# Expert blocks of a mixture-of-experts stage: gathered token rows in six buffers in place of three

## The chip, the cores and the metric

The kernel runs on one core of a Trainium2 chip. The metric is the device time of one execution in microseconds (us); below, KB means 1024 bytes and MB a million, as the profile counts them.

## The reference

The reference is a chain of eight layers on N = 3125 nodes of D = 256 features, all in float32: four graph layers over 50000 edges, and four mixture-of-experts layers. Three of the experts' layers matter here. Cut down, the first of them is:

```python
# layer L0_ffn: 16 experts, 2 chosen, width 512 (F)
topk_vals, topk_idx = jax.lax.top_k(x @ gate_w + gate_b, 2)
topk_w = jax.nn.softmax(topk_vals, axis=-1)
h = relu(einsum('bsh,ehf->bsef', x, w1) + b1)
expert_out = einsum('bsef,efh->bseh', h, w2) + b2
moe = sum(topk_w[..., None] * take(expert_out, topk_idx))
```

L2_ffn has 8 experts of width 1024, of which each token takes one, up to a capacity of 489 tokens an expert. L3_ffn has 6 experts, two chosen, with three matrices each (256 to 256 to 256 to 256).

## The kernel before

The kernel does not compute every expert for every token. `route` sorts the (token, expert) pairs by expert into blocks of BR = 250 rows, each block of one expert, and writes two lists: `token_i`, which token's row each slot of a block takes, and `to_i`, where its answer goes. `block_experts` (line 1442) then works through the blocks. It is called three times, and the text calls its stages by letters:

- **stage A**, L0_ffn: 40 blocks, weights of 1026 KB a block, stage start near 1584 us of the span;
- **stage B**, L2_ffn: 16 blocks, weights of 2052 KB a block, near 5272 us;
- **stage C**, L3_ffn: 30 blocks, weights of 770 KB a block, near 6390 us.

In each stage a block of 250 rows is two half-blocks of 125 (TB = 2), and each engine runs its own program, held together by semaphores:

- **SyncE** (line 1494) loads for block n the weights `w` and the second bias `b2` (125 KB, broadcast over the partitions) into one of three buffers. From block 3 on it first waits until block n-3 has its answers (`o_done`).
- **GpSimd** (line 1627) gathers and scatters. `gather(n)` (line 1637) issues two indirect DMAs, 125 rows of 1 KB each, from `tokens` in DRAM to `rows`. The buffer is chosen by n modulo R = 3, and from block 3 on the gather first waits until block n-3 has been transposed (`t_mm`). The scatter of block n (line 1655; line 1660 in stage B, a plain DMA) writes the two halves of `y` to `answered`, after `o_done` of block n. The loop over n (line 1649) is: gather block n + R, wait for `o_done` of block n, scatter block n. In stage A the last nine turns of the loop each also issue up to three small indirect DMAs `order_d`, 25 in all (line 1665); they belong to a sort for a later layer.
- **TensorE** (line 1504) transposes a block's rows (`turn`, line 1511, waits for `rows_in`), multiplies with the first matrix (`up`, line 1525, waits for `w_in`), in stage C with the middle one (`middle`, line 1534), and with the last (`down`, line 1544). It runs ahead: the order is

```python
for n in range(blocks):
    if FM: middle(n)
    if n + 1 < blocks: up(n + 1)
    if n + 2 < blocks: turn(n + 2)
    down(n)
```

- **ScalarE** evicts `hid` and `mid` (lines 1566, 1577); **VectorE** copies the transposed rows out of PSUM to `xT` (line 1587) and adds `b2` to the product to make `y` (line 1595). `y` has two buffers: VectorE waits until the scatter of block n-2 has landed (`stored`).

So the gather of block n+4 stands on GpSimd directly behind the scatter of block n, which waits for `down(n)`; and `down(n+2)` stands on TensorE behind `turn(n+4)`, which waits for that gather.

Of the kernel before, what the change touches and what calls it, by code (L numbers as in the profile page):

```python
# [17 lines left out]
N, D, E = 3125, 256, 50000  # L18
P = 125
# [18 lines left out]
def stage(k):  # L38

    return Stage(k)  # L40
# [336 lines left out]
def make_records(k, fld, slot_i, attr_t, m_w1, m_b1, m_w2, m_b2, noise):  # L377

    nc = k.nc
    K1, GE = 50, G * 128  # L380
    R = 3
    with stage(k) as s:
        attr = s.sb("attr", [K1, R, GE])
        pos, hid = s.sb("pos", [128, 2, 2, GE]), s.sb("hid", [128, 2, 2, GE])
        hs = s.sb("hs", [128, 2, 2, GE])
        rec = s.sb("rec", [128, R, G, RW])
        w1, b1 = s.sb("w1", [K1, D]), s.sb("b1", [128, 2])
# [3 lines left out]
            s.sem(n) for n in ("w_in", "hid_mm", "hid_act", "hid_exp", "hid_ln", "hs_done", "fil_mm", "rec_done"))  # L391
        attr_in, sent = ([s.sem(f"{n}{j}") for j in range(R)] for n in ("attr_in", "sent"))
        noise_in = s.sem("noise_in")
        with s.block() as block:
            @block.sync
            def _(sp):
# [7 lines left out]
                for g in range(NGR):  # L404
                    if g >= R:
                        sp.wait_ge(hid_mm, 2 * (g - R) + 2)
                    sp.dma_start(attr[:, g % R, :], attr_t[:, g * GE:(g + 1) * GE]).then_inc(attr_in[g % R], 16)
# [672 lines left out]
BR = 250  # L1080
# [361 lines left out]
def block_experts(k, table, token_i, result, block_i, x, blocks, sort=False, shift=None, to_i=None):  # L1442
# [5 lines left out]
    nc = k.nc  # L1448
    FC = x.f // 128
    FM = 2 if x.wm is not None else 0  # L1450
    TB = BR // P
    R = 3
    SEMS = 2
    EACH = 3
    FROM = blocks - NT // EACH - 1
# [9 lines left out]
    cleared = 0 if to_i is not None else 1  # L1465
    last_fill = lambda n: fill["mid", n, FM - 1] if FM else fill["up", n, FC - 1]
    with stage(k) as s:
        rows = s.sb("rows", [P, R, TB, D])
        xT = s.sb("xT", [128, 2, 2, BR])
        w, b2 = s.sb("w", [128, R, x.width]), s.sb("b2", [P, R, D])  # L1470
        part = lambda n, at, to: w[:, n % R, at:to]
# [8 lines left out]
        if FM:  # L1480
            mid = s.sb("mid", [128, 2, FM, BR])
        ps_t, ps_h, ps_o = s.ps("ps_t", [128, 2, 512]), s.ps("ps_h", [128, 4, 512]), s.ps("ps_o", [P, 2, 512])
        w_in, rows_in = ([s.sem(f"{n}{j}") for j in range(R)] for n in ("w_in", "rows_in"))
        stored = [s.sem(f"stored{b}") for b in range(2)]
        t_mm, t_ev, h_mm, h_sb, o_mm, o_done, made = (s.sem(n) for n in ("t_mm", "t_ev", "h_mm", "h_sb", "o_mm", "o_done", "made"))
        if sort:
# [5 lines left out]
        with s.block() as block:  # L1492
# [10 lines left out]
            @block.tensor  # L1503
            def _(pe):
                def turn(n):
                    pe.wait_ge(rows_in[n % R], 16 * TB * (n // R + 1))
                    if n >= 2:
                        pe.wait_ge(t_ev, n - 1)
                    for t in range(TB):
                        for half in range(2):  # L1510
                            ins = nc.tensor.transpose(ps_t[:, n % 2, half * BR + t * P:half * BR + (t + 1) * P], rows[:, n % R, t, half * 128:(half + 1) * 128], k.ident[0:P, 0:P])
                    ins.then_inc(t_mm, 1)

                def free(at):
                    if at >= 4:
                        pe.wait_ge(h_sb, at - 3)

                def up(n):
                    pe.wait_ge(w_in[n % R], 16 * SEMS * (n // R + 1))
                    pe.wait_ge(t_ev, n + 1)  # L1520
                    for f in range(FC):
                        at = fill["up", n, f]
                        free(at)
                        for c in range(2):
                            ins = nc.tensor.matmul(ps_h[:, at % 4, 0:BR], w1(n, c, f), xT[:, n % 2, c, :], start=c == 0, stop=c == 1)  # L1525
                        ins.then_inc(h_mm, 1)

                def middle(n):
                    pe.wait_ge(h_sb, fill["up", n, FC - 1] + 1)
                    for f in range(FM):  # L1530
                        at = fill["mid", n, f]
                        free(at)
                        for c in range(FC):
                            ins = nc.tensor.matmul(ps_h[:, at % 4, 0:BR], wm(n, c, f), hid[:, n % 2, c, :], start=c == 0, stop=c == FC - 1)
                        ins.then_inc(h_mm, 1)

                def down(n):
                    pe.wait_ge(h_sb, last_fill(n) + 1)
                    last, count = (mid, FM) if FM else (hid, FC)
                    for t in range(TB):  # L1540
                        if n:
                            pe.wait_ge(o_done, 2 * (n - 1) + t + 1)
                        for c in range(count):
                            ins = nc.tensor.matmul(ps_o[:, t, 0:D], last[:, n % 2, c, t * P:(t + 1) * P], w2(n, c), start=c == 0, stop=c == count - 1)
                        ins.then_inc(o_mm, 1)

                turn(0)
                turn(1)
                up(0)
                for n in range(blocks):  # L1550
                    if FM:
                        middle(n)
                    if n + 1 < blocks:
                        up(n + 1)
                    if n + 2 < blocks:
                        turn(n + 2)
                    down(n)

            @block.scalar
            def _(act):  # L1560
                def up(n):
                    act.wait_ge(w_in[n % R], 16 * SEMS * (n // R + 1))
                    for f in range(FC):
                        at = fill["up", n, f]
                        act.wait_ge(h_mm, at + 1)
                        nc.scalar.activation(hid[:, n % 2, f, :], ps_h[:, at % 4, 0:BR], x.func, bias=b1(n, f)).then_inc(h_sb, 1)  # L1566
# [15 lines left out]
            def _(dve):  # L1582
# [6 lines left out]
                def answers(n):  # L1589
                    dve.wait_ge(w_in[n % R], 16 * SEMS * (n // R + 1))  # L1590
                    if n // 2 + cleared:
# [36 lines left out]
            @block.gpsimd  # L1628
            def _(pool):
                if sort:  # L1630
                    nc.gpsimd.iota(ids[:], [[P, NT]], base=0, channel_multiplier=1).then_inc(ready, 1)
                    nc.gpsimd.memset(before[:], 1.0).then_inc(ready, 1)
                    pool.wait_ge(ready, 2)
                    nc.gpsimd.affine_select(out=before[:], in_=before[:], compare_op=ALU.is_gt, fill=0.0, base=0,
                                            pattern=[[-1, P]], channel_multiplier=1).then_inc(ready, 1)

                def gather(n):
                    if n >= R:
                        pool.wait_ge(t_mm, n - R + 1)
                    for t in range(TB):  # L1640
                        nc.gpsimd.indirect_dma_start(rows[:, n % R, t, :], None, table, bass.IndirectOffsetOnAxis(token_i[:, TB * n + t:TB * n + t + 1], 0)).then_inc(rows_in[n % R], 16)

                for n in range(R):
                    gather(n)
                pool.wait_ge(made, 1)
                for lo, hi in SPLIT[0:2 * cleared]:
                    for b in range(2):
                        pool.dma_start(result[blocks * BR + b * P + lo:blocks * BR + b * P + hi, :], zero[lo:hi, :]).then_inc(stored[b], 16)
                for n in range(blocks):
                    if n + R < blocks:  # L1650
                        gather(n + R)
                    pool.wait_ge(o_done, 2 * n + 2)
                    if to_i is not None:
                        for t in range(TB):
                            nc.gpsimd.indirect_dma_start(result, bass.IndirectOffsetOnAxis(to_i[:, TB * n + t:TB * n + t + 1], 0), y[:, n % 2, t, :], None,
                                                         bounds_check=2 * N - 1, oob_is_err=False).then_inc(stored[n % 2], 16)
                    else:
                        to = result[n * BR:(n + 1) * BR, :].rearrange("(t p) f -> p t f", p=P)
                        for lo, hi in SPLIT:
                            pool.dma_start(to[lo:hi], y[lo:hi, n % 2, :, :]).then_inc(stored[n % 2], 16)  # L1660
                    if sort and n >= FROM:
                        if n == FROM:
                            pool.wait_ge(ranked, 1)
                        for t in range(EACH * (n - FROM), min(EACH * (n - FROM + 1), NT)):
                            nc.gpsimd.indirect_dma_start(k.order_d, bass.IndirectOffsetOnAxis(k.rank_i[:, t:t + 1], 0), ids[:, t:t + 1], None).then_inc(ordered, 16)
                if sort:
                    pool.wait_ge(ordered, 16 * NT)
                for b in range(2):
                    pool.wait_ge(stored[b], 32 * (blocks // 2 + cleared))
# [1629 lines left out]
```

## Time and profile before

| | |
|---|---|
| median of 3 runs | 6747.97 us (6741.45 to 6748.28) |
| the profiled execution's own time | 6698.96 us |
| its span, first to last instruction | 6697.1 us |
| mean granted TensorE clock | 0.785 of full |
| busy: TensorE matmuls, VectorE, ScalarE, GpSimd | 67%, 50%, 38%, 46% of the span |
| mean DMA rate over the span | 109 GB/s |
| stages A, B, C, first gather to last scatter | about 385, 255 and 265 us |

Shares of the span are means over some thirty stages with different limits, so they say little on one stage. The rows further down are of the three stages alone. In a timeline a row gives the start, the length, the engine and line, and in brackets how long the engine had been idle before, and what ended that. A DMA instruction on GpSimd is the writing of its descriptors; the transfer goes on after it. "PEclk" is the clock granted to TensorE as a share of full speed.

### The profile page before, as it was taken

The numbers are of one execution on the slowest core, as the hardware profiler recorded it, in microseconds if no ns is written. First come the engines' busy times: TensorE is split into PE (matmuls) and PEld (weight loads), VectorE is DVE, ScalarE is ACT, GpSimd is POOL, SyncE is SP. The second block draws the span as 40 slices with busy tenths as digits, with TensorE's granted clock in tenths as the row PEclk, the third lists the DMA queues.
The fourth block names the chain that finished last, engine by engine and source line by source line (L and its number), as shares of the span: only waits on it lengthen the run. The fifth ranks groups of instructions, "written<-read, shape, count | busy, mean of one in ns | idle before, by whom it ended". The sixth has DMA issues, their size and how long they took to land. (4 is left out here: it accounts for less than half of the span.)

```text
span 6697.1 us, 62301 instructions
## 1 busy us (share of the span) xinstructions
PE 4506.5 (67%) x16614; PEld 3138.6 (47%) x16614; DVE 3363.6 (50%) x7195; ACT 2539.8 (38%) x5493; POOL 3081.5 (46%) x2991
## 2 busy tenths in 40 slices
PE   4799945556954777545556676996777592555665
PEld 2466634345743555212245343774555581333454
DVE  2344435554625666679744565225666315454522
ACT  2577723331212233355432443223333122666511
POOL 3276766652653666235500652004665124666244
PEclk7899966766986666679977788997777696677878
DMA  4433343334644555224330221004555353666245
GB/s 115 128 105 103 107 89 92 91 81 116 201 136 114 140 139 138 58 82 132 107 79 9 51 47 29 14 3 124 140 143 126 115 168 102 183 188 182 66 140 168
DMA packets 464743, 727.93 MB, mean 109 GB/s; under 512 B 173990, under 2 KB 334801, under 8 KB 453972
## 3 DMA queue, kind: packets, MB, share of 16 engines
q1 hardware_dynamic: 299372, 388.69, 20.0%
q0 software_dynamic: 161520, 330.66, 18.8%
q10 hardware_dynamic: 3530, 4.89, 0.2%
q8 instruction: 129, 2.11, 0.1%
q14 instruction: 192, 1.57, 0.1%
HBM read 592.07 MB, written 139.85 MB: 109 GB/s over the span
## 5 line engine op out<-in xcount | busy, mean ns | idle before, releaser
L593 PE MATMUL ps<-msg,same 128*125 128x256 f32 (+2 forms) x3328 | 1343.0, 548 | 883.9 <-issue 397.7
L593 PEld LDWEIGHTS ps<-msg,same 128*125 128x125 f32 x3328 | 773.1, 260 | 1297.8 <-issue 787.2
L569 POOL DMA_INDIRECT msg<-d_gat,src_i x832 | 794.1, 954 | 430.9 <-issue 197.0
L482 POOL DMA_INDIRECT rec<-rec,slot_i x391 | 415.8, 1063 | 299.5 <-PE ps_f L424 121.2
L569 POOL DMA_INDIRECT msg<-d_lin,src_i x416 | 394.2, 948 | 267.8 <-issue 101.9
L569 POOL DMA_INDIRECT msg<-rel_rows,src_rel x416 | 399.4, 960 | 213.5 <-issue 98.3
L645 ACT ACTIVATE same<-off 128x500 f32<-128x500 f32 x208 | 128.9, 620 | 865.8 <-PE ps L593 455.2
L424 PE MATMUL ps_f<-w,hs 128*128 128x256 f32 x1568 | 391.0, 406 | 27.1 <-DVE hs L462 26.3
L639 ACT ACTIVATE off<-ramp_r,minus_lo 128x125 f32<-128x125 f32 x1248 | 390.6, 384 | 10.9 <-PEq L58 10.9
L424 PEld LDWEIGHTS ps_f<-w,hs 128*128 128x128 f32 x1568 | 308.7, 202 | 145.8 <-DVE hs L462 74.9
L1566 ACT ACTIVATE hid<-ps_h,w 128x250 f32<-128x250 f32 x348 | 163.5, 470 | 531.8 <-PE ps_h L1525 508.6
L2642 PE MATMUL ps_y<-pr,ident 128*128 128x447 f32 (+1 forms) x448 | 212.6, 600 | 208.9 <-DVE pr L2693 208.9
L1525 PE MATMUL ps_h<-xT,w 128*128 128x250 f32 x1392 | 323.3, 387 | 28.0 <-DMA b<-in_L_ffn_b 27.8
L580 PEld LDWEIGHTS ps_v<-vt,pick 125*128 125x128 f32 x1664 | 290.0, 251 | 105.9 <-issue 86.5
L2632 POOL TENSOR_TENSOR dB<-rows,u 128x894 f32<-128x894 f32 (+1 forms) x112 | 215.3, 1924 | 230.0 <-DVE hh L2684 162.2
L2811 POOL DMA_INDIRECT msg<-d_small,idx x256 | 242.3, 946 | 161.0 <-DVE weighed L2914 84.9
L580 PE MATMUL ps_v<-vt,pick 125*128 x1664 | 271.2, 295 | 49.7 <-DVE pick L688 37.8
L1525 PEld LDWEIGHTS ps_h<-xT,w 128*128 128x128 f32 x1392 | 271.1, 196 | 70.5 <-DMA b<-in_L_ffn_b 37.1
L462 DVE SCALAR_TENSOR_TENSOR hs<-hid,pos 128x1024 f32<-128x1024 f32 x98 | 120.1, 1225 | 355.6 <-ACT hid L452 258.6
L2828 PE MATMUL ps<-spread,oh_lo 128*125 128x500 f32 x512 | 253.6, 654 | 66.6 <-DVE spread L2920 66.6
L717 DVE TENSOR_TENSOR agg_m<-agg_m,ps 125x256 f32 x416 | 174.7, 420 | 204.8 <-DMA got<-answered,slot_i 90.4
L717 DVE TENSOR_TENSOR x<-x,ps 125x256 f32 x416 | 174.6, 420 | 203.8 <-DMA rec<-blank,pad_i 75.1
(594 smaller groups left out, 9209.3 us busy)
## 6 DMA issues: line engine op xcount, KB each, us to landing
lo_rows<-lo_r SPq DMA_DIRECT2D x208, 256.0 KB
fil<-rec SPq DMA_DIRECT2D x104, 512.0 KB
rows<-bc_d SPq DMA_DIRECT2D x96, 447.0 KB
w<-in_L_ffn_packed SPq DMA_DIRECT2D x40, 1026.0 KB
w<-in_L_ffn_packed SPq DMA_DIRECT2D x16, 2052.0 KB
w<-in_L_ffn_packed SPq DMA_DIRECT2D x30, 770.0 KB
rel_rows<-row SPq DMA_DIRECT2D x25, 896.0 KB
lo_rows<-ffn_lo_r SPq DMA_DIRECT2D x32, 500.0 KB
```

What stands on the lines that cost most here:

```text
L424: ins = nc.tensor.matmul(ps_f[:, g % 2, j, :], hs[:, g % 2, c, j * 128:(j + 1) * 128], w2[:, c, :], start=c == 0, stop=c == 1)
L482: nc.gpsimd.indirect_dma_start(k.rec, bass.IndirectOffsetOnAxis(slot_i[0:rows, c:c + 1], 0), rec[0:rows, g % R, j, :], None).then_inc(sent ...
L569: nc.gpsimd.indirect_dma_start(msg[:, g % R, j, :], None, table, bass.IndirectOffsetOnAxis(idx[:, n:n + 1], 0)).then_inc(msg_in[g % R], 16)
L580: ins = nc.tensor.matmul(ps_v[:, g % 2, j * H2:(j + 1) * H2], pick[0:P, g % 2, j * 128:(j + 1) * 128], vt[:, ds(t, 1), :].rearrange("p t h ...
L593: nc.tensor.matmul(ps[:, j, 0:width], same[:, g % 2, j, :], msg[:, g % R, j, 0:width], start=True, stop=True).then_inc(mm, 1)
L639: ins = nc.scalar.activation(off[:, b, j, :], k.ramp_r1[:], ACT.Abs, bias=k.minus_lo1[:, n:n + 1])
L717: nc.vector.tensor_tensor(into, into, ps[:, j, 0:width], ALU.add).then_inc(added, 1)
L1525: ins = nc.tensor.matmul(ps_h[:, at % 4, 0:BR], w1(n, c, f), xT[:, n % 2, c, :], start=c == 0, stop=c == 1)
L2632: nc.gpsimd.tensor_tensor(dB[:, n % 3, :, 0:hi - lo], both(rows[:, n % R, 0, 0:hi - lo], hi - lo), u[:, :, lo:hi], ALU.mult).then_inc(ins_ ...
L2642: ins = nc.tensor.matmul(ps_y[:, h, 0:size(n)], k.ident[:], pr[:, n % 2, h, 0:size(n)], start=st == 0, stop=st == SN - 1)
L2811: nc.gpsimd.indirect_dma_start(msg[:, g % R, j, :], None, table, bass.IndirectOffsetOnAxis(idx[:, n:n + 1], 0)).then_inc(msg_in[g % R], 16)
L2828: nc.tensor.matmul(ps[:, 0:NT * W], oh_lo[:, g % 2, j, :], spread[:, g % 2, j, :], start=False, stop=False).then_inc(mm, 1)
```

## The change

`rows` gets a buffer count of its own, RR = 6, with a semaphore for each buffer, and everything that indexed `rows` or `rows_in` by R uses RR. The weights keep R = 3. On GpSimd six blocks are gathered ahead of the loop, and turn n of the loop gathers block n + 6, in place of n + 3, ahead of the scatter of block n. The buffer's wait becomes that for the transposition of block n - 6 of the gather's block. `rows` takes 12 KB of each partition in place of 6.

```diff
     R = 3
+    RR = 6
...
-        rows = s.sb("rows", [P, R, TB, D])
+        rows = s.sb("rows", [P, RR, TB, D])
...
-        w_in, rows_in = ([s.sem(f"{n}{j}") for j in range(R)] for n in ("w_in", "rows_in"))
+        w_in, rows_in = [s.sem(f"w_in{j}") for j in range(R)], [s.sem(f"rows_in{j}") for j in range(RR)]
...
-                    pe.wait_ge(rows_in[n % R], 16 * TB * (n // R + 1))
+                    pe.wait_ge(rows_in[n % RR], 16 * TB * (n // RR + 1))
...
                 def gather(n):
-                    if n >= R:
-                        pool.wait_ge(t_mm, n - R + 1)
+                    if n >= RR:
+                        pool.wait_ge(t_mm, n - RR + 1)
...
-                for n in range(R):
+                for n in range(RR):
                     gather(n)
...
                 for n in range(blocks):
-                    if n + R < blocks:
-                        gather(n + R)
+                    if n + RR < blocks:
+                        gather(n + RR)
                     pool.wait_ge(o_done, 2 * n + 2)
```

The order changes on GpSimd alone. At the start of stage A its program before is this (`rows<-tokens` is a gather of half a block, `answered<-y` a scatter of half a block):

```order
L1641 DMA rows<-tokens,token_i_16 125x256 x8
L1655 DMA answered<-y,to_i_16 6250x256 x2
L1641 DMA rows<-tokens,token_i_16 125x256 x2
L1655 DMA answered<-y,to_i_16 6250x256 x2
L1641 DMA rows<-tokens,token_i_16 125x256 x2
```

and with the change (its lines are one further down):

```order
L1642 DMA rows<-tokens,token_i_16 125x256 x14
L1656 DMA answered<-y,to_i_16 6250x256 x2
L1642 DMA rows<-tokens,token_i_16 125x256 x2
L1656 DMA answered<-y,to_i_16 6250x256 x2
L1642 DMA rows<-tokens,token_i_16 125x256 x2
```

Seven blocks are gathered ahead of the first scatter where four were; after that, scatters and gathers alternate as before. The end of stage C on GpSimd before:

```order
L1655 DMA answered<-y,to_i_6 6250x256 x2
L1641 DMA rows<-tokens,token_i_6 125x256 x2
L1655 DMA answered<-y,to_i_6 6250x256 x2
L1641 DMA rows<-tokens,token_i_6 125x256 x2
L1655 DMA answered<-y,to_i_6 6250x256 x8
```

and with the change:

```order
L1656 DMA answered<-y,to_i_6 6250x256 x2
L1642 DMA rows<-tokens,token_i_6 125x256 x2
L1656 DMA answered<-y,to_i_6 6250x256 x2
L1642 DMA rows<-tokens,token_i_6 125x256 x2
L1656 DMA answered<-y,to_i_6 6250x256 x14
```

The last gather stands ahead of the last seven blocks' scatters, where it stood ahead of the last four.

## Rows read from the trace of the kernel before

**Rows 1.** Waits of stage A, 1584 to 1968: us in total, times, longest.
```profile
PE ps_t L1511 <- DMA rows<-tokens,token_i: 35.8, 9, 15.2
PE ps_h L1525 <- DMA b<-in_L_ffn_b: 27.8, 16, 9.4
```
**Rows 2.** Waits of stage B, 5272 to 5530.
```profile
PE ps_t L1511 <- DMA rows<-tokens,token_i: 26.5, 2, 21.7
```
**Rows 3.** Waits of stage C, 6389 to 6662.
```profile
POOL answered L1655 <- DVE y L1595: 83.0, 17, 12.0
PE ps_t L1511 <- DMA rows<-tokens,token_i: 69.2, 15, 15.3
```
**Rows 4.** Windows: PE, PEld, DVE, ACT, POOL busy (count), PEclk, DMA share, GB/s.
```profile
1643.00:1880.00 237.00, 218.27 (x1030) 184.73 (x1028) 140.92 (x238) 53.15 (x114) 140.51 (x115) 0.98 0.66 199
1880.00:1970.00 90.00, 61.14 (x264) 50.96 (x264) 17.89 (x28) 13.16 (x28) 67.17 (x53) 0.88 0.38 101
6418.00:6655.00 237.00, 179.89 (x793) 152.88 (x791) 42.91 (x85) 53.57 (x114) 136.53 (x112) 0.91 0.53 161
...
5282.00:5292.00 10.00, 0.99 (x4) 0.71 (x4) 0.00 (x0) 0.00 (x0) 1.23 (x3) 0.50 1.02 325
```
**Rows 5.** Timeline of stage C, TensorE: turn, middle and up.
```profile
6444.52 1.10 PE L1511 MATMUL ps_t<-ident,rows 125*128 125x125 f32 x4 [4.03 <-DMA rows<-tokens,token_i]
...
6461.40 1.08 PE L1511 MATMUL ps_t<-ident,rows 125*128 125x125 f32 x4 [4.00 <-DMA rows<-tokens,token_i]
...
6465.29 1.85 PE L1534 MATMUL ps_h<-hid,w 128*128 128x250 f32 x8
...
6470.83 1.85 PE L1534 MATMUL ps_h<-hid,w 128*128 128x250 f32 x8
6472.52 1.85 PE L1525 MATMUL ps_h<-xT,w 128*128 128x250 f32 x8
```
**Rows 6.** Timeline of stage C, GpSimd: first scatter, one round, last scatter.
```profile
6418.55 1.24 POOL L1655 DMA_INDIRECT answered<-y,to_i  x1 [12.04 <-DVE y L1595]
...
6449.86 1.23 POOL L1655 DMA_INDIRECT answered<-y,to_i  x1 [4.99 <-DVE y L1595]
...
6452.91 1.23 POOL L1641 DMA_INDIRECT rows<-tokens,token_i  x1 [0.30 <-issue]
6454.44 1.22 POOL L1641 DMA_INDIRECT rows<-tokens,token_i  x1 [0.30 <-issue]
6455.97 1.23 POOL L1655 DMA_INDIRECT answered<-y,to_i  x1 [0.30 <-issue]
...
6652.51 1.19 POOL L1655 DMA_INDIRECT answered<-y,to_i  x1 [1.56 <-DVE y L1595]
```
**Rows 7.** Timeline of stage C, SyncE's queue: a load of weights.
```profile
6466.10 0.35 SPq L1500 DMA_DIRECT2D w<-in_L_ffn_packed  x1
```
**Rows 8.** Timeline of stage A, TensorE: turns of blocks 4, 5, 33 and 35.
```profile
1635.95 0.59 PE L1511 MATMUL ps_t<-ident,rows 125*128 125x125 f32 x4
...
1643.22 0.59 PE L1511 MATMUL ps_t<-ident,rows 125*128 125x125 f32 x4
...
1875.53 0.59 PE L1511 MATMUL ps_t<-ident,rows 125*128 125x125 f32 x4
...
1898.29 1.09 PE L1511 MATMUL ps_t<-ident,rows 125*128 125x125 f32 x4 [4.60 <-DMA rows<-tokens,token_i]
```
**Rows 9.** Timeline of stage A, GpSimd: scatter of block 31, its gather, the end.
```profile
1880.96 1.22 POOL L1655 DMA_INDIRECT answered<-y,to_i  x1 [1.46 <-DVE y L1595]
...
1884.01 1.19 POOL L1665 DMA_INDIRECT order_d<-ids,rank_i  x1 [0.30 <-issue]
...
1968.99 1.19 POOL L1665 DMA_INDIRECT order_d<-ids,rank_i  x1 [0.30 <-issue]
```
**Rows 10.** Timeline of a graph layer behind stage A, GpSimd: gathers in a row.
```profile
2088.33 1.19 POOL L569 DMA_INDIRECT msg<-d_gat,src_i  x1 [13.05 <-POOLq L58]
...
2122.44 0.95 POOL L569 DMA_INDIRECT msg<-d_gat,src_i  x1 [0.30 <-issue]
```

More of the change, by code:

```diff
@@ L1510, in turn @@
                         for half in range(2):
-                            ins = nc.tensor.transpose(ps_t[:, n % 2, half * BR + t * P:half * BR + (t + 1) * P], rows[:, n % R, t, half * 128:(half + 1) * 128], k.ident[0:P, 0:P])
+                            ins = nc.tensor.transpose(ps_t[:, n % 2, half * BR + t * P:half * BR + (t + 1) * P], rows[:, n % RR, t, half * 128:(half + 1) * 128], k.ident[0:P, 0:P])
                     ins.then_inc(t_mm, 1)
@@ L1637, in gather @@
                 def gather(n):
-                    if n >= R:
-                        pool.wait_ge(t_mm, n - R + 1)
+                    if n >= RR:
+                        pool.wait_ge(t_mm, n - RR + 1)
                     for t in range(TB):
-                        nc.gpsimd.indirect_dma_start(rows[:, n % R, t, :], None, table, bass.IndirectOffsetOnAxis(token_i[:, TB * n + t:TB * n + t + 1], 0)).then_inc(rows_in[n % R], 16)
-                for n in range(R):
+                        nc.gpsimd.indirect_dma_start(rows[:, n % RR, t, :], None, table, bass.IndirectOffsetOnAxis(token_i[:, TB * n + t:TB * n + t + 1], 0)).then_inc(rows_in[n % RR], 16)
+                for n in range(RR):
                     gather(n)
```

## The prediction

> **What bounds the kernel now.** The three stages are read in three views. First the waits of each stage, for what TensorE waits. In stage C it waited 69.2 us in 15 places for gathered rows [rows 3], the first, 15.3 us, being the stage's start; that leaves 53.9 us. In stage A it waited 35.8 us for rows and 27.8 us for the load of weights and bias [rows 1]. In stage B both waits for rows lie at the start [rows 2], before any buffer is used again, and nothing else waits for a load.
>
> Second the timeline of stage C, for the loop that makes these waits. TensorE waits at every second turn, and the waits stand 6461.40 - 6444.52 = 16.88 us apart, two blocks [rows 5]. Follow one round. The turn of block 6 at 6444.52 lets `down(4)` run; its answers let GpSimd start the scatter of block 4 at 6449.86; behind the two scatters the gather of block 8 is issued, 6452.91 and 6454.44; it lands at 6461.4, where the turn of block 8 had waited for it [rows 5, 6]. So 5.3 us of work, 5.8 us of descriptor writing (two scatters and two gathers of 1.22 us with 0.30 us between) and 5.7 us of flight make up the loop, and it closes over two blocks only because the gather behind the scatter of block n is that of block n+4.
>
> Third the windows. In stage C the DMA engines are busy 0.53 of the time at 161 GB/s, GpSimd 136.5 of 237 us, and TensorE is granted 0.91 of its 2.4 GHz [rows 4]. Nothing is full. At a stage's start they are full: 1.02 at 325 GB/s [rows 4].
>
> **Stage C, the loop's new length.** Behind the scatter of block n now stands the gather of block n+7, needed five turns later. The loop of about 17 us closes over five blocks, 3.4 us a block: it binds nothing. What is late next? Three candidates:
> - TensorE's own work: two middles without a wait between are 6470.83 - 6465.29 = 5.54 us apart [rows 5].
> - GpSimd: two scatters and two gathers take 6455.97 - 6449.86 = 6.11 us [rows 6]. No more is to be issued than before, so this is a floor as long as gathers remain.
> - The weights: a load is issued when block n-3 is answered. One issued at 6466.10 was in place for the up at 6472.52 with no wait [rows 5, 7], so it takes 6.4 us at most. With a block of 5.54 us the load has just about these 6.4 us; with 6.11 us, about 7.
>
> From the first scatter at 6418.55 to the last block's at 6652.51 there are 234.0 us for 29 blocks, 8.07 each [rows 6]. Floors: TensorE 29 x 5.54 = 160.7; GpSimd 58 scatters and the 46 gathers of blocks 7 to 29, 104 x 1.53 = 159. So no more than 73 us can be gained. GpSimd paces the 23 rounds that hold gathers, for it may fall only two blocks behind before VectorE waits for a free `y`; in the last six TensorE does. I add 0.2 us a block for weights that come late: between nothing and what stage A shows, whose 27.8 us less the 9.4 of the start are 0.5 us a block over some 36 blocks [rows 1], with larger loads. That is 23 x 6.3 + 6 x 5.6 = 179 us: **stage C gains 55 us** (30 to 73).
>
> The clock is part of this. Behind each 4 us wait the turn takes 1.08 us, where an undisturbed one takes 0.59 [rows 5, 8]; that is the 1.2 GHz level. Without such waits this goes too, and the 5.54 us hold it already.
>
> **Stage A, the middle.** From the turn of block 5 to that of 33 a block takes (1875.53 - 1643.22) / 28 = 8.30 us, against 1643.22 - 1635.95 = 7.27 us of TensorE's work [rows 8]. The difference is the weights. Each load still starts when block n-3 is answered, and the scatter and gather issued at that moment are as many as before. I cost it at nothing. The few short waits for rows in there may turn into waits for weights.
>
> **Stage A, the tail.** From block 31 on three `order_d` stand behind each scatter, and the next gather behind those. So the turn of block 35 waited 4.60 us [rows 8], and three later ones about as long or less. GpSimd works from 1880.96 to 1970.2, 89.2 us [rows 9], with only short waits. With the change two blocks' gathers (38 and 39) are left after the scatter of block 31, where five were: 18 scatters, 25 `order_d`, 4 gathers, 47 issues of 1.5 us, 71 us. That would gain 18. TensorE has eight blocks to do in that time, 58 us at 7.27 or 66 at the middle's 8.30, so it nearly fits: **the tail gains 17 us** (8 to 20).
>
> **The starts.** In each stage six gather issues now follow the first six at once instead of after the first turn: 3 x 250 KB more in flight while the DMA engines are full. At 325 GB/s [rows 4] that is 2.4 us of their time. It stands behind the first rows in the same queue, and the first weights were asked for earlier. Cover: the engines are slack once the first block runs. If it fails, each stage starts up to 2.4 us later, 7 in all; I take 0. That the queue takes so many is shown behind stage A: 28 gathers in a row, 2088.33 to 2122.44, each 0.30 us behind the other [rows 10]. In stage B the rest is TensorE's own work: 0, between +1 and -5.
>
> **Against it, the sharing of the engines.** Row: with loads and gathers in flight together the first turn of stage B waited 21.7 us, that of stage A 15.2 [rows 1, 2], and stage B's loads are twice as large. So a gather in flight and a load do slow each other. The Trainium skill, DMA: Bandwidth & Descriptors, section Queues, rings and completion order, says that each engine goes round-robin between the queue rows that have work, one packet at a time. By that rule a gather nobody is waiting for takes its share from the load that is urgent; the case that makes of it is the first rival below.
>
> **The sum.** 55 + 17 + 0 = 72 us of the profiled execution's 6698.96, so 6627. That execution stands 49 us (0.7%) under the median of the runs; the same share of the median is 6747.97 x (1 - 72/6699) = 6675.5, or **6676 us**.
>
> **Rivals.**
> - *Weights take the rows' place* (0.22). Every block of stage C loses to late weights what a block of stage A's middle loses, 8.30 - 7.27 = 1.03 us [rows 8]: 23 x 7.14 + 6 x 6.57 = 204, a gain of 30, and the tail of A gives 10. Result 6708. For it: three buffers of weights stay, and the load's time of up to 6.4 us is near its window. Against: stage C loads 895 KB a block where A loads 1151, and has the middle as further window; there is no wait for weights in C now.
> - *Everything hides* (0.08): GpSimd's and TensorE's floors are reached, 73 + 20 = 93 us, 6654.
> - *No change* (0.05). The rows come late for a reason other than the buffer, say a queue that delivers at its own pace; then the waits of C return after the lead of seven blocks is used up. Against: the 16.88 us round closes in its parts, and those gathers flew when a 0.53 busy DMA had room.
> - *Slower* (0.03). The gathers in flight push each load of stage A later by their own bytes, 250 KB at some 300 GB/s, 0.83 us, in 40 blocks: 33 us. It decides if the load's landing, not `o_done`, sets the pace there, and C gains nothing because its loads slip by the same. With the tail's gain that is +16, 6764. Against: the number of gathers issued per block, and their place behind the scatter, stay as they are.
>
> **How the numbers follow.** Forecast 0.62, the rivals 0.22, 0.08, 0.05 and 0.03. A measurement of this kernel can tell 0.2%, 13.5 us, from no change. Faster by more: 0.62 + 0.22 + 0.08 = 0.92; within: 0.05; slower: 0.03. The range takes in the first two rivals and 10 us on either side: 6645 to 6718.
>
> **What would show it.** In the profile after: in stage C no waits of the turns for rows but the start's; GpSimd busy some 0.75 to 0.8 of the stage, gaps of 0.30 us; the last scatter some 55 us nearer the first; a granted clock near 1; DMA share near 0.7 at 200 GB/s or more; a few waits of `up` for the bias or weights. In stage A the middle unchanged at 8.3 us a block, the tail free of waits for rows. The prediction is wrong if `up` waits over 1 us a block in stage C, if the middle of A moves by more than 0.3 us a block, or if a start grows by more than 3 us.

## The result, and the profile after

The changed kernel takes 6663.19 us (median of 4 runs, 6653.67 to 6669.11) against 6748.12 us: 84.9 us less, a ratio of 0.9874 with a 95% interval of 0.9857 to 0.9892. Forecast were 6676 us and 72 us.

The two profiled spans, 6697.1 and 6656.1 us, differ by 41 us only. The profiled execution of before was 49 us under its median; the one after, 6659.38 us, is 4 us under its own. So the gain is read stage by stage, not from the spans. On GpSimd, stage A from first gather to the end of the last issue, B and C to its start:

| stage | before | after | gain |
|---|---|---|---|
| A, in all | 385.9 | 359.9 | 26.0 |
| A, turn of block 5 to turn of block 33 | 232.3 | 224.2 | 8.1 |
| A, scatter of block 31 to the end | 89.2 | 72.6 | 16.6 |
| B | 253.0 | 254.7 | -1.7 |
| C, in all | 264.1 | 202.6 | 61.5 |
| C, first scatter to last block's scatter | 234.0 | 174.6 | 59.4 |

The three stages give 85.8 us, 0.9 more than the difference of the medians. That they meet so closely is in part luck. The two spans differ by 41 us, so the rest of the kernel reads 45 us longer in the profile after, and 19.6 of these lie ahead of stage A's first gather (at 1584.27 before and 1603.85 after), where the change has no part. And A's middle, with 8.1 us, does not come out again when the changed kernel is profiled a second time, below; the medians there give 75.4 us.

The waits of stage C after the change (engine, what it waited for: us in total, times, longest), to be held against [rows 3]:

```profile
POOL answered L1656 <- DVE y L1596: 24.1, 9, 5.7
PE ps_t L1512 <- DMA rows<-tokens,token_i: 16.6, 2, 14.7
PE ps_h L1526 <- DMA b<-in_L_ffn_expert_b: 10.4, 9, 2.3
DVE y L1596 <- DMA answered<-y,to_i: 3.1, 1, 3.1
```

The turns wait for rows twice, both at the start; of the 53.9 us behind the first wait 2.0 are left. GpSimd, which had waited 83.0 us for answers, waits 24.1. Two small waits are new: `up` for weights and bias, and VectorE for a `y` whose scatter had not landed.

GpSimd in stage C after the change, timeline: one round from the scatter of block 0, the two longer gaps with the scatters of blocks 16 and 22, the first later one that waits, and the scatter of the last block:

```profile
6435.43 1.24 POOL L1656 DMA_INDIRECT answered<-y,to_i  x1 [5.65 <-DVE y L1596]
6436.97 1.22 POOL L1656 DMA_INDIRECT answered<-y,to_i  x1 [0.30 <-issue]
6438.49 1.22 POOL L1642 DMA_INDIRECT rows<-tokens,token_i  x1 [0.30 <-issue]
6440.02 1.22 POOL L1642 DMA_INDIRECT rows<-tokens,token_i  x1 [0.30 <-issue]
6441.54 1.23 POOL L1656 DMA_INDIRECT answered<-y,to_i  x1 [0.30 <-issue]
...
6533.78 1.23 POOL L1656 DMA_INDIRECT answered<-y,to_i  x1 [0.92 <-DVE y L1596]
...
6571.44 1.23 POOL L1656 DMA_INDIRECT answered<-y,to_i  x1 [1.31 <-DVE y L1596]
...
6583.79 1.20 POOL L1656 DMA_INDIRECT answered<-y,to_i  x1 [3.49 <-DVE y L1596]
...
6610.00 1.19 POOL L1656 DMA_INDIRECT answered<-y,to_i  x1 [1.57 <-DVE y L1596]
```

Four issues make a round of 6.11 us with nothing between them but 0.30 us. Block 22 has the last gathers behind it; one more round of 6.11 us brings the scatter of block 23 at 6577.55. In these 142.1 us the two gaps shown at 6533.78 and 6571.44 are the only ones over 0.31 us; that is 6.18 us a round for 23 rounds. Once the gathers are used up GpSimd waits again, and the last six blocks come every (6610.00 - 6577.55) / 6 = 5.41 us, near TensorE's own 5.54.

The windows after (us, PE, PEld, DVE, ACT and POOL busy with counts, granted clock, DMA share, GB/s): A's middle, A's tail, C from first to last scatter; before they were those of [rows 4]:

```profile
1661.60:1885.80 224.20, 208.59 (x1010) 177.79 (x1009) 139.21 (x235) 52.64 (x112) 137.49 (x113) 1.00 0.69 205
1891.20:1963.80 72.60, 53.92 (x261) 46.27 (x259) 17.79 (x27) 13.16 (x28) 58.54 (x47) 0.93 0.40 113
6435.40:6611.20 175.80, 162.00 (x790) 138.66 (x788) 42.81 (x85) 53.11 (x113) 128.03 (x105) 0.99 0.72 212
```

In C the DMA share has gone from 0.53 to 0.72, the rate from 161 to 212 GB/s, the granted clock from 0.91 to 0.99. GpSimd is busy 128 of 176 us, 0.73. That hides how full it is: in a round without a wait it is busy 4.9 of 6.11 us, 0.80, the rest being its four gaps of 0.30 us. The clock is a good part of the gain: for nearly the same matmuls (790 and 793) TensorE is busy 162.0 us in place of 179.9 [rows 4]. So some 17 of the 59.4 us are quicker matmuls, and the rest is idle time that went.

The tail of stage A: the scatter of block 31, and the last issue.

```profile
1891.19 1.23 POOL L1656 DMA_INDIRECT answered<-y,to_i  x1 [1.88 <-DVE y L1596]
...
1962.57 1.19 POOL L1666 DMA_INDIRECT order_d<-ids,rank_i  x1 [0.30 <-issue]
```

The 47 issues counted in the forecast stand in the window above as x47, and the turns behind block 31 have no wait for rows.

The waits of `up` in stage C can be held against their loads. The loads of blocks 4 and 5, and the `up` of each:

```profile
6440.21 0.35 SPq L1501 DMA_DIRECT2D w<-in_L_ffn_packed  x1
...
6445.75 0.35 SPq L1501 DMA_DIRECT2D w<-in_L_ffn_packed  x1
```

```profile
6447.49 1.96 PE L1526 MATMUL ps_h<-xT,w 128*128 128x250 f32 x8 [0.69 <-DMA b<-in_L_ffn_expert_b]
...
6454.03 1.96 PE L1526 MATMUL ps_h<-xT,w 128*128 128x250 f32 x8 [0.73 <-DMA b<-in_L_ffn_expert_b]
```

These loads, with the bias that is asked for right behind the weights, took 7.3 and 8.3 us, where the one read before the change took 6.4 at most [rows 5, 7].

### The profile page after: what moved, and what is told of

Its sections match the earlier page's. It is cut to its first block and busy times, and to the rows that moved or that the text cites. A ratio compares the mean times of both kernels' runs of the same rounds, so it can differ in the third digit from the quotient of the medians.

```text
span 6656.1 us, 62301 instructions
## 1 busy us (share of the span) xinstructions
PE 4476.5 (67%) x16614; PEld 3128.7 (47%) x16614; DVE 3365.6 (51%) x7195; ACT 2539.2 (38%) x5493; POOL 3079.0 (46%) x2991
## 5 line engine op out<-in xcount | busy, mean ns | idle before, releaser
L593 PE MATMUL ps<-msg,same 128*125 128x256 f32 (+2 forms) x3328 | 1345.4, 550 | 916.0 <-issue 374.3
L717 DVE TENSOR_TENSOR agg_m<-agg_m,ps 125x256 f32 x416 | 174.6, 420 | 212.0 <-DMA got<-answered,slot_i 101.3
L717 DVE TENSOR_TENSOR agg_c<-agg_c,ps 125x260 f32 x416 | 176.5, 424 | 186.8 <-PE ps L593 66.2
```

The lines of the kernel that those rows point to most:

```text
L593: nc.tensor.matmul(ps[:, j, 0:width], same[:, g % 2, j, :], msg[:, g % R, j, 0:width], start=True, stop=True).then_inc(mm, 1)
L717: nc.vector.tensor_tensor(into, into, ps[:, j, 0:width], ALU.add).then_inc(added, 1)
```

## The experiments

Two groups of four ran, each on a chip of its own. The kernel before took 6694.6 us on the first and 6172.2 us on the second, so whole kernels are compared with before on the same chip, and across the groups by their stages. All start from the changed kernel. One without the change kept is named so. "Stage C" is first gather to last issue on GpSimd; the changed kernel has 202.6 us. Before has one profile alone, so every gain of a stage leans on it. Sums of the three stages and medians agree in some runs (76.2 and 75.4 us for the changed kernel again) and part by up to 12 us in others (80.3 and 68.6 with four buffers, 70.7 and 59.7 with six in stage C alone).

**Four buffers in place of six.**

```diff
-    RR = 6
+    RR = 4
```

> Four buffers of rows in place of six. Theory (the loop): with k buffers the gather behind the scatter of block n is that of block n+k+1, so the round of about 17 us closes over k-1 blocks, 5.6 us a block with four, under GpSimd's 6.11. So stage C keeps nearly all of its gain: 175 to 180 us from first to last scatter (175 with six, 234 with three), and no wait of a turn for rows behind the start. Stage A's tail has 8 gathers left behind block 31's scatter instead of 4, 77 us instead of 73. In all 75 to 85 us faster than before, where six give 85. Rival (jitter): landings vary so much that a lead of one block is worth little; then stage C stays over 195 us with waits for rows, and the whole gains under 60.

Measured: 68.6 us faster than before, ratio 0.9900 (0.9883 to 0.9916). Stage C took 203.0 us, first to last block's scatter 6573.11 - 6398.55 = 174.6 us, as with six. (Four profiles with six buffers of rows in C, three of weights and the whole scatter read 171.9 to 174.6, so a microsecond or two says nothing.) Its waits for loads and its two end scatters:

```profile
PE ps_t L1512 <- DMA rows<-tokens,token_i: 17.1, 2, 15.2
PE ps_h L1526 <- DMA b<-in_L_ffn_expert_b: 10.9, 11, 3.0
```

```profile
6398.55 1.24 POOL L1656 DMA_INDIRECT answered<-y,to_i  x1 [10.44 <-DVE y L1596]
...
6573.11 1.19 POOL L1656 DMA_INDIRECT answered<-y,to_i  x1 [1.56 <-DVE y L1596]
```

The loop's theory holds: 17 us over three blocks is already under GpSimd's round, and no turn behind the start waits for rows. A's tail read 80.1 us, where 77 were expected, between 72.6 and 89.2. The whole fell short of the 75 to 85 expected; its interval includes them only in part, and the tail is the only stretch that reads clearly worse than with six.

**Six buffers for the weights too.**

```diff
-    R = 3
+    R = 6 if x.f < 1024 else 4
```

> Six buffers of rows, and six for the weights in stages A and C (four in stage B). Theory (GpSimd paces stage C): the waits of up for weights, 10.4 us in C and 20 us in A behind the start, go; stage C stays at 172 to 175 us from first to last scatter, since two scatters and two gathers still take 6.11 us; stage A's middle goes from 8.0 to about 7.3 us a block, 20 us, and the starts may grow by 2 to 5 us because more weights are asked for at once. In all about 100 us faster than before. Rival (weights pace stage C): C falls to 165 us or less, and the whole gains 110 or more. Second rival (the DMA engines are the limit in A): A's middle stays at 8.0 and nothing is gained there.

Measured: 98.7 us faster, ratio 0.9847 (0.9831 to 0.9864). The waits of stage C:

```profile
DVE y L1596 <- DMA answered<-y,to_i: 58.0, 20, 5.9
POOL answered L1656 <- DVE y L1596: 21.6, 8, 9.7
PE ps_t L1512 <- DMA rows<-tokens,token_i: 18.4, 2, 14.4
PE ps_o L1545 <- DVE y L1596: 7.6, 6, 1.6
```

and its first and last block's scatter:

```profile
6378.59 1.24 POOL L1656 DMA_INDIRECT answered<-y,to_i  x1 [9.65 <-DVE y L1596]
...
6546.90 1.19 POOL L1656 DMA_INDIRECT answered<-y,to_i  x1 [1.57 <-DVE y L1596]
```

No wait for weights is left, and 168.3 us remain: 6.3 us less than with three, and 4 less than the lower end of what I had expected. TensorE and VectorE now run up against the two buffers of `y`, that is against the scatters, 58 us in 20 places, and GpSimd has no gap over 0.31 us in its first 23 rounds. So GpSimd's issues pace stage C up to block 23, at 6.11 us a block, only 1.6 us less in all than with three buffers of weights. The other 4.6 us come behind it: TensorE, no longer held up by weights, is ahead when the gathers end, and the last six blocks come every (6546.90 - 6519.09) / 6 = 4.64 us in place of 5.41. My 172 to 175 us amount to TensorE's own time for these. Late weights thus cost some 6 us, most of it as a lead that TensorE did not have. The rival, C at 165 us or less, fell. In stage A the middle went to 203.5 us, 7.27 a block, which is TensorE's work to the hundredth: the weights paced it, and the DMA engines were not the limit. Stage B took 260.3 us, 5.7 more than the changed kernel, all of it ahead of its first scatter, where four loads of 2 MB are asked for at once.

**Six buffers in stage C alone.**

```diff
-    RR = 6
+    RR = 6 if FM else 3
```

> Six buffers of rows in stage C only, three in A and B. Theory: the gain of the change is the sum of its stages, so this gives C's 61 us alone: 55 to 65 us faster than before, and stage A reads as before, 386 us from first gather to last issue, with its middle at 8.3 us a block. Rival: A's middle was faster by chance; then stage A's middle reads 8.0 us here too, and the whole gains about 70.

Measured: 59.7 us faster, ratio 0.9916 (0.9899 to 0.9933). Stage C took 202.3 us, 61.8 less than before, as forecast. Stage A has the code of before in it and its tail read 91.1 us, yet its middle read 221.9, 7.93 a block: here the rival was right about the middle, though not about a whole gain of 70. The 59.7 us are near C's gain alone, but with A's middle 10 us quicker the stages of this profile sum to 70.7, so the whole does not show it by itself; its interval is 45 to 68 us.

**Half of the scatters left out in stage C.**

```diff
+    PARTS = 1 if FM else 2
...
-                        dve.wait_ge(stored[n % 2], 32 * (n // 2 + cleared))
+                        dve.wait_ge(stored[n % 2], 16 * PARTS * (n // 2) + 32 * cleared)
...
-                        for t in range(TB):
+                        for t in range(PARTS):
                             nc.gpsimd.indirect_dma_start(result, ...)
```

The last wait for `stored` counts in the same way.

> Six buffers of rows; in stage C the second half of each block's answers is not written, so its scatter is one DMA instead of two. That leaves out half of the scatter of layer L3_ffn. Theory (GpSimd paces stage C): its round falls from 6.11 to 4.6 us, so TensorE's 5.54 us a block and the late weights remain: stage C 163 to 168 us from first to last scatter in place of 175. Rival (weights pace stage C): the round is not GpSimd's, and C stays within 3 us of 175, less what 128 KB a block less traffic gives.

Measured: 79.5 us faster than before, ratio 0.9880 (0.9864 to 0.9897). Stage C, first to last block's scatter:

```profile
6406.61 1.24 POOL L1657 DMA_INDIRECT answered<-y,to_i  x1 [6.24 <-DVE y L1597]
6412.15 1.23 POOL L1657 DMA_INDIRECT answered<-y,to_i  x1 [1.26 <-DVE y L1597]
...
6572.39 1.19 POOL L1657 DMA_INDIRECT answered<-y,to_i  x1 [3.05 <-DVE y L1597]
```

165.8 us in place of 174.6, and GpSimd waits longer than 0.31 us ahead of the scatter in every round, by the profile in 27 of 30 for the answers. With one issue less a round, the pace passed to TensorE (160.7 us) and a few late weights (4.8 us in all). That is the second sign that the pace was GpSimd's. Some of the 8.8 us may be due to the bytes left out; this run does not part the two. Stage A, which has the change in full here, read 8.30 us a block in its middle.

**The changed kernel again**, on the second chip.

> The changed kernel itself once more, beside the ones it is compared with. Theory: its gain is C's 60 us and the tail of A's 17 us, near 75 to 85 us; the middle of stage A reads anywhere between 7.9 and 8.3 us a block, since the same code has read 8.01 and 8.30 and code without the change 8.30 and 7.93. Rival: the change speeds A's middle, which then reads 8.0 or less again.

Measured: 75.4 us faster, ratio 0.9881 (0.9864 to 0.9897). C took 201.6 us, A's tail 73.5, B 253.9. A's middle read 232.3 us, 8.30 a block, as before the change. With this the seven readings of that stretch with three buffers of weights and the gather directly behind its scatter are 8.30 and 7.93 with three buffers of rows, 7.91 with four, and 8.01, 8.30, 8.30 and 8.29 with six. So the 8.1 us in the table of the result can't be told from the spread of equal code, and nothing shows a gain in A's middle. Why the readings fall near 7.95 or near 8.30 is open.

**Three buffers, the gather's place alone.**

```diff
-    RR = 6
+    RR, AHEAD = 3, 5
...
-                for n in range(RR):
+                for n in range(AHEAD):
                     gather(n)
...
-                    if n + RR < blocks:
-                        gather(n + RR)
+                    if n + AHEAD < blocks:
+                        gather(n + AHEAD)
```

> Three buffers of rows as before, but the gather of block n+5 stands in front of the scatter of block n (it waits for the turn of block n+2, which stands on TensorE in front of down n). Theory (only the place of the gather against the scatter counts, since the buffer was free long before): the gather no longer stands behind its scatter by two blocks; the round is turn, two issues of 1.5 us, up to 5.7 us of flight, back to the turn three blocks on, about 10 us over three blocks. Stage C then reads as with six buffers, 174 to 178 us from first to last scatter, and the whole gains nearly as much: 65 to 85 us. Rival (the buffers count): with three, TensorE waits for rows again and C stays over 195 us.

Measured: 65.7 us faster than before, ratio 0.9895 (0.9878 to 0.9912). Stage C took 202.2 us, 0.6 more than with six buffers on this chip. Its first scatter came 29.4 us behind its first gather, where the changed kernel has 26.6 on this chip and 29.0 in the run with six in stage C alone; the stretch from there to the last reads 171.3 us, under the 174 to 178 expected, as that run's does with 171.9. The waits for rows in C:

```profile
PE ps_t L1512 <- DMA rows<-tokens,token_i: 16.6, 2, 15.0
```

So three buffers were enough in C: the old kernel did not lack memory, its gather stood behind a scatter that it had no need to wait for. In stage A the middle read 8.73 us a block, 244.4 us against 232.3, outside the 7.91 to 8.30 of the seven. GpSimd now waits there for turns, but that does not hold up a scatter: in each such place the scatter behind the gathers still had to wait for its answers. One of them:

```profile
1512.64 1.22 POOL L1642 DMA_INDIRECT rows<-tokens,token_i  x1 [4.34 <-PE ps_t L1512]
...
1517.17 1.22 POOL L1656 DMA_INDIRECT answered<-y,to_i  x1 [1.79 <-DVE y L1596]
```

What is longer there is the wait of `up` for weights and bias, 26.3 us in place of 19.6. That is 6.7 of the 12.1 us; why this order should make it longer, and what the rest is, stays open. The whole is 10 us behind six buffers, within what the two intervals leave open.

**`order_d` out of stage A.**

```diff
-                    if sort and n >= FROM:
-                        ...
-                            nc.gpsimd.indirect_dma_start(k.order_d, ...)
 ...
 def fetch_pairs(...):
+            if sort:
+                @block.gpsimd
+                def _(pool):
+                    ...
+                    for t in range(NT):
+                        nc.gpsimd.indirect_dma_start(k.order_d, ...)
```

> Six buffers of rows, and the 25 small order_d scatters issued in the next stage, where GpSimd has nothing to do, instead of stage A's last nine blocks. Theory (GpSimd's issues bound A's tail, 47 of 1.5 us): without them the tail has 22 issues, 33 us, and TensorE bounds it: from the scatter of block 31 to the last scatter's end about 8 x 8.0 + 3 = 67 us in place of 71; so 4 to 8 us more gain than the changed kernel has, if the next stage does not grow. Rival: the DMA traffic of order_d moves into the next stage, which reads and writes there, and makes it longer by what is gained.

Measured: 90.0 us faster than before, ratio 0.9853 (0.9833 to 0.9873), 14.6 us more than the changed kernel on the same chip. Stage A took 356.4 us in place of 371.3, 14.9 less, and its tail 59.5. I had expected 67: the tail ran at 7.3 us a block, not at the middle's 8.3. The next stages took 99.0 us from the first load of `got` to the reduction that ends the layer's front, against 100.4, so nothing was given back. In the tail of the changed kernel the pace was GpSimd's. The first products of the tail show one thing more; the last gather was issued at 1720.47:

```profile
1706.99 3.65 PE L1537 MATMUL ps_h<-xT,w 128*128 128x250 f32 x16 [0.81 <-DMA b<-in_L_ffn_b]
...
1715.43 3.65 PE L1537 MATMUL ps_h<-xT,w 128*128 128x250 f32 x16 [0.91 <-DMA b<-in_L_ffn_b]
...
1722.80 3.54 PE L1537 MATMUL ps_h<-xT,w 128*128 128x250 f32 x16
...
1730.07 3.62 PE L1537 MATMUL ps_h<-xT,w 128*128 128x250 f32 x16
```

While gathers are issued, `up` comes 8.44 us behind the last and waits for its load; behind the last gather it comes every 7.3 us, with three buffers of weights as before.

**Both: six buffers of weights in A and C, three in B, `order_d` moved** (as in the run before).

```diff
-    R = 3
+    R = 6 if x.f < 1024 else 3
```

> Six buffers of rows, six of weights in stages A and C, three in B (whose start grew by 5.7 us with four), and order_d moved to the next stage. Theory: A's middle at TensorE's 7.27 us a block, and its tail too, so stage A takes 323 to 328 us from first gather to last scatter (337 with six weights alone, 360 with the change); B as before the change, 253 to 255; C 199 to 203 us. In all 112 to 122 us faster than before. Rival: with the tail rid of order_d nothing more comes, because the tail was TensorE's already: 100 to 107 us.

Measured: 6049.11 us against 6172.2 us, 123.1 us faster, ratio 0.9806 (0.9789 to 0.9822): the best of all, 48 us under the changed kernel. A took 319.6 us, B 253.5, C 195.7, so A and C each came out some 3 us under what was expected. The rival, 100 to 107 us, fell. A's middle and C from first to last scatter, windows:

```profile
1469.30:1672.80 203.50, 203.50 (x1010) 179.69 (x1009) 138.31 (x231) 52.63 (x112) 133.85 (x111) 1.00 0.77 229
5830.80:6000.60 169.80, 158.84 (x790) 138.90 (x788) 40.33 (x85) 53.10 (x113) 128.99 (x106) 1.00 0.72 209
```

In A's middle the profile has TensorE busy throughout, at full clock, with the DMA engines at 229 GB/s.

## Why the prediction was right

**What bound stage C** was named rightly: the round through scatter, gather and flight that closed over two blocks. Four buffers, where it closes over three, gave all of C's gain; three buffers with the gather two places earlier gave it too. The part I had not drawn from my own reading is the latter. The loop is one of order, not of memory, and two buffers fewer or a line moved would have done in C.

**What bounds it now** was named rightly too: GpSimd's four issues, floor 6.11 us. I had 6.3 for 23 rounds and 5.6 for six blocks, 179 us; it was 6.18 and 5.41, 174.6. The 0.2 us a block for late weights was too much: `up` waited 10.4 us in nine places, but GpSimd, a little behind TensorE, kept issuing through most of these. Six buffers of weights priced them at 6.3 us in all. So C gained 61.5 us, of which 2.1 at its start, and not 55. The 73 us given as the most that could be had took each engine's total alone. The prediction's own rounds, 23 x 6.11 + 6 x 5.54 = 173.8 us, leave 60, and 59.4 were measured; 65.7 came only with six buffers of weights, which let TensorE be ahead when the gathers ended. The sign for GpSimd, busy 0.75 to 0.8, came out at 0.73.

**Stage A's tail** gained 16.6 us, forecast 17, and for the reason given: moving `order_d` away showed that GpSimd sets its pace. What I used as TensorE's lower end there, 58 to 66 us, was nearer 58: 59.5 without `order_d`.

**Stage A's middle** was costed at nothing. In the profile it gained 8 us, 0.29 us a block, just inside the 0.3 that I had allowed. Readings of equal code spread as far, so nothing is the right value as far as can be told. That the weights pace it is shown by 7.27 us a block with six buffers of them.

**The starts and stage B** cost nothing that can be told apart: A's first scatter came 29.6 us behind its first gather in place of 30.5, C's 26.5 in place of 28.7, and B's stage was 1.7 us longer, inside its bounds. With six buffers of weights A's first scatter came at 33.0 and 32.8 us in the two runs, where three give 29.4 to 31.4, so loads asked for all at once do cost some 2 us at that start. In C the same two runs read 30.5 and 27.1, against 26.5 to 29.4, which shows nothing clear.

**The first rival**, weights in the rows' place, came in part: such waits appeared in stage C, where there had been none, while the DMA rate rose to 212 GB/s. The loads took 7.3 and 8.3 us where 6.4 had been enough, and in stage A of the run with `order_d` moved no load but one was late, by 0.36 us, once the gathers were over. This agrees with a gather in flight taking its share from a load. The Trainium skill has that as a rule (DMA: Bandwidth & Descriptors, section Queues, rings and completion order: round-robin between the queue rows with work). It is not shown apart from the rest: in C the loads also follow each other more closely than before, and behind the last gather in A the DMA engines have less to carry in all; either alone could do the same. Its size was the point: 6 us in C, not 30. Nothing in the traces speaks for the rival "no change" or for the one that ended slower.

The sum, 55 + 17 + 0 = 72, was thus short of the 85 measured by 6.5 in C; in the profile the rest is A's middle, whose 8 us no one could have forecast, and 1.3 us of A's start, with the 1.7 us of B and 0.4 of the tail against them. On the second chip, where A's middle read as before, the whole gained 75.4 us. So some 78 us, C and the tail, are shown stage by stage; how much of the 85 is theirs, and how much is the spread of the rest of the kernel, the runs leave open.

## What to carry to other kernels

When an engine that gathers also scatters in program order, write down how many blocks the loop scatter, gather, flight, use closes over, and divide its length by them; then ask whether the gather needs that scatter at all, since a place in the order may be worth as much as buffers. Count the issues of such an engine with their gaps, for at 0.80 busy it was full, and over a stage that held six rounds without gathers it read 0.73. When one wait goes, price the next floors first (here 5.54 us, 6.11 us and the weights): they said beforehand that 60 to 73 of 234 us were to be had, and they named the next gains, six buffers of weights and 25 small scatters moved.

## What was not expected

- The kernel before took 6748, 6695 and 6172 us in three groups of runs, the last two on chips of their own, while the expert stages of the changed kernel read alike: C 202.6 and 201.6 us, B 254.7 and 253.9. A good half of the difference lies in the graph layers: ahead of the products of line 593 TensorE sat idle 916.0 us in the changed kernel's first profile and 602.1 in its second, on the chip of 6172. Why is open.
- A stretch paced by loads of weights, A's middle, reads 7.93 and 8.30 us a block in two executions of equal code, and 8.01 and 8.30 in two others; one paced by TensorE reads 7.266 and 7.267. A few microseconds in the first kind of stretch are no evidence.
